# A macaron block on one core: key products of rows 6 to 15 as two f16 products, new places for part of the work, weights fetched earlier

## What is computed

```python
def ffn(x):                                # on layernorm(x); all weights are -1, 0 or 1, with a scale per output
    h = silu(tlin(x, w1, w1_s)) * tlin(x, w2, w2_s)          # 256 -> 1024
    h = gelu(tlin(h, h1, h1_s)); h = gelu(tlin(h, h2, h2_s)) # 1024 -> 1024, twice
    return tlin(h, w3, w3_s)                                 # 1024 -> 256

def attention(x):                          # on layernorm(x), and normed once more inside
    q, k, v, beta_pre = split(normed @ w_qkvb + b_qkvb, 4)
    k = k / max(norm(k), 1e-6); beta = sigmoid(beta_pre)
    for t in range(T):                     # one state S of 16x16 for each head
        S = S + (beta[t] * (v[t] - S @ k[t])) outer k[t]
        o[t] = S @ q[t]
    return x + o @ w_out + b_out

x = x + 0.5 * ffn(layernorm(x)); x = x + attention(layernorm(x)); x = x + 0.5 * ffn(layernorm(x))
```

## Time and profile before

| | |
|---|---|
| median of 3 runs | 1837.86 us (1837.82 to 1837.88) |
| the profiled execution's own time | 1835.54 us |
| its span, first to last instruction | 1833.8 us |
| PE busy | 1764.8 us, 96% |
| PE weight loads busy | 1063.5 us, 58% |
| DVE busy | 1249.4 us, 68% |
| POOL busy | 1075.2 us, 59% |
| ACT busy | 989.1 us, 54% |
| granted PE clock | 0.997 of full speed |

### The profile page before, as it was taken

The page is one execution under the profiler, slowest core; times in us unless marked ns, Lnnn a source line. Parts: engine busy times, 40 slices in busy tenths (PEclk is TensorE's granted clock), DMA queues, the critical chain, the costliest instruction groups (busy, mean ns, idle before and its releaser), DMA issues.

```text
span 1833.8 us, 28121 instructions
## 1 busy us (share of the span) xinstructions
PE 1764.8 (96%) x9674; PEld 1063.5 (58%) x9674; DVE 1249.4 (68%) x2873; ACT 989.1 (54%) x1904; POOL 1075.2 (59%) x1314
## 2 busy tenths in 40 slices
PE   5999999999999999999999999999999899999999
PEld 3865555555655555555555556555555555555588
DVE  5365687777776876767677686767868777778441
ACT  4555464555555454655545465554646454645454
POOL 3553574647465655747466574755756575657563
PEclk8999999999999999999999999999999999999999
DMA  7100000000000000000000000000000000000000
GB/s 273 56 1 1 1 1 1 1 1 1 1 1 1 24 1 12 13 1 2 0 24 1 1 1 1 24 1 1 1 1 1 1 1 12 1 1 13 1 13 13
DMA packets 5260, 23.05 MB, mean 13 GB/s; under 512 B 640, under 2 KB 1664, under 8 KB 3584
## 3 DMA queue, kind: packets, MB, share of 16 engines
q1 hardware_dynamic: 5120, 21.26, 3.1%
HBM read 17.06 MB, written 4.19 MB: 12 GB/s over the span
## 4 chain that ended last, share of the span: by engine, by line
PE 80%; DVE 7%; issue 6%; POOL 4%; ACT 3%; DMA 0%; DVEq 0%; POOLq 0%; SPq 0%; ACTq 0%
PE ffn_bank L1030 46%; PE ffn_bank L1013 10%; PE att_bank L1078 6%; PE att_bank L1050 5%; PE att_bank L1068 5%; PE state_bank L1086 2%; PE ln_bank L981 2%; POOL hid_lo L520 2%; PE att_bank L1065 1%; POOL pairs L549 1%; PE att_bank L1066 1%; PE att_bank L1095 1%; ACT hid L637 1%; DVE roots L756 1%; DVE qk_u L842 1%
## 5 line engine op out<-in xcount | busy, mean ns | idle before, releaser
L1030 PE MATMUL ffn_bank<-hid_hi,w_sb 128*128 128x512 f16 (+1 forms) x2592 | 893.6, 356 | 11.7 <-DVE w_sb L727 5.6
L1030 PE MATMUL ffn_bank<-hid_lo,w_sb 128*128 128x512 f16 (+1 forms) x2592 | 893.4, 356 | 0.0
L520 POOL TENSOR_TENSOR hid_lo<-hid,hid_hi 128x512 f16<-128x512 f32 (+1 forms) x432 | 454.4, 1068 | 385.0 <-ACT hid_hi L613 383.8
L1030 PEld LDWEIGHTS ffn_bank<-hid_hi,w_sb 128*128 128x128 f16 x2592 | 262.9, 101 | 222.3 <-issue 18.3
L549 POOL TENSOR_TENSOR pairs<-KQ 128x32 f32<-128x32 f32 (+15 forms) x496 | 324.6, 667 | 113.5 <-DVE KQ L805 57.2
L1030 PEld LDWEIGHTS ffn_bank<-hid_lo,w_sb 128*128 128x128 f16 x2592 | 254.1, 98 | 228.4 <-issue 26.7
L613 ACT CAST hid_hi<-hid 128x512 f16<-128x512 f32 (+1 forms) x432 | 231.5, 572 | 32.9 <-DVE hid L778 32.5
L637 ACT ACTIVATE hid<-ffn_bank,par_sb 128x512 f32<-128x512 f32 (+1 forms) x288 | 169.0, 637 | 148.3 <-PE ffn_bank L1030 146.8
L1013 PE MATMUL ffn_bank<-xn_hi,w_sb 128*128 128x512 f16 (+1 forms) x576 | 200.2, 357 | 13.9 <-DVE w_sb L727 6.3
L557 POOL TENSOR_TENSOR pairs_lo<-pairs,pairs_hi 128x32 f16<-128x32 f32 (+15 forms) x256 | 180.5, 711 | 52.1 <-ACT pairs_hi L685 47.2
L1013 PE MATMUL ffn_bank<-xn_lo,w_sb 128*128 128x512 f16 (+1 forms) x576 | 200.0, 357 | 0.0
(11 more groups left out here) (82 smaller groups left out, 2092.7 us busy)
## 6 DMA issues: line engine op xcount, KB each, us to landing
NK<-in_w SPq DMA_DIRECT2D x11, 1024.0 KB, 5.0
X<-in_x SPq DMA_DIRECT2D x7, 512.0 KB, 3.6
out<-X SPq DMA_DIRECT2D x7, 512.0 KB, 2.6
wqkvb_sb<-in_wqkvb SPq DMA_DIRECT2D x1, 1024.0 KB, 10.1
X<-in_x SPq DMA_DIRECT2D x2, 256.0 KB, 2.7
out<-X SPq DMA_DIRECT2D x2, 256.0 KB, 2.1
wout_sb<-in_wout SPq DMA_DIRECT2D x1, 256.0 KB, 11.2
par_sb<-in_par SPq DMA_DIRECT2D x1, 24.0 KB, 2.5
```

Of the source, the lines that this page charges most:

```text
L520: pool.tensor_tensor(hid_lo[layer % 2][:, m, call.cols], hid[:, u % 3, call.cols], hid_hi[layer % 2][:, m, call.cols], ALU.subtract).then_ ...
L1030: mm = nc.tensor.matmul(ffn_ps(call, j), weight(name, kk, 2 * pair + i), v[:, kk, cols], start=kk == 0 and part == 0, stop=kk == KT_FF - 1 ...
```

## The change

1. kk rows 6 to 15 are made as qk rows are: a high part by ACT, a low part by POOL, and two f16 products on PE, with a new f16 matrix `head_minus16`. Rows 1 to 5 stay in f32.
2. The place of each pairs, high and low instruction is no longer a fixed distance from PE's tick alone. A loop over all products puts the pairs of a cut product 9 ticks ahead, the high part 4 and the low part 3, and later where the product before it or the owner of its buffer would come later (`MAKE_AT`, `HIGH_AT`, `LOW_AT`).
3. Tables move: the last chunk's opening product from tick 66 to 69 and its update from 81 to 82, the tenth qk row from 26 to 23, the output projection from 53 to 52, one step of the attention norm, and four feed-forward norms by 1 to 3 ticks. ACT copies the keys 8 ticks after a chunk opens, not 6.
4. At the start SP no longer waits for x: three pieces of weights follow the parameters at once, and the second half of x comes after them. The second layer norm moves to slots 26 to 66 of the first call. DVE casts a piece after every second `mix`, and PE waits for a piece of h1, h2 or w3 only at the slot that uses it. ACT calls Sqrt once on a constant before anything else.

```diff
-FIRST_TICK = 2
+FIRST_TICK = 0
-E_RETR = [0, 22, 44, 66]
-E_STATE = [13, 35, 58, 81]
+E_RETR = [0, 22, 44, 69]
+E_STATE = [13, 35, 58, 82]
-E_OUT = 53
+E_OUT = 52
-E_QK = [1, 4, 6, 10, 12, 14, 17, 19, 21, 26, 28, 32, 34, 36, 39, 41]
+E_QK = [1, 4, 6, 10, 12, 14, 17, 19, 21, 23, 28, 32, 34, 36, 39, 41]
-PAIR_LEAD = {"kk": 4, "qk": 9}
+PAIR_LEAD = {"whole": 4, "half": 9}
-SPLIT = {use: q for q, use in enumerate(u for u in DOTS if u[0] == "qk")}
+SPLIT_FROM = {"kk": 6, "qk": 0}
+SPLIT = {use: q for q, use in enumerate(u for u in DOTS if u[2] >= SPLIT_FROM[u[0]])}
...
+MAKE_AT, HIGH_AT, LOW_AT = {}, {}, {}
+for _q, _dot in enumerate(DOTS):
+    _last = DOTS[_q - 1] if _q else None
+    _at = max(WHEN[_dot] - PAIR_LEAD["half" if _dot in SPLIT else "whole"], FIRST_TICK - TICKS, MAKE_AT.get(_last, -TICKS))
+    if _q >= PAIR_BUFFERS:
+        _owner = DOTS[_q - PAIR_BUFFERS]
+        _at = max(_at, LOW_AT[_owner] if _owner in SPLIT else WHEN[_owner])
+    MAKE_AT[_dot] = _at
+    if _dot in SPLIT:
+        _i = SPLIT[_dot]
+        _at = max(WHEN[_dot] - HIGH_LEAD, _at, HIGH_AT.get(SPLITS[_i - 1], _at) if _i else _at)
+        if _i >= HALF_BUFFERS:
+            _at = max(_at, WHEN[SPLITS[_i - HALF_BUFFERS]] + 3)
+        HIGH_AT[_dot] = _at
+        LOW_AT[_dot] = max(WHEN[_dot] - LOW_LEAD, _at, LOW_AT.get(SPLITS[_i - 1], _at) if _i else _at)
...
-LN_SECOND = dict(sum=2, mean=4, square=6, sq_sum=8, var=10, root=12, apply=30, low=34)
+LN_SECOND = dict(sum=26, mean=30, square=32, sq_sum=36, var=40, root=43, apply=62, low=66)
...
+            load_head(0)
+            sp.dma_start(par_sb[:, :], par).then_inc(par_loaded, 16)
             for i in range(W_PIECES):
                 stage_piece(i)
+                if i == W_STAGES - 1:
+                    load_head(1)
...
+            act.wait_ge(eps_ready, 2)
+            act.activation(gate[:, 0, 0:1], eps[:, 0:1], ACT.Sqrt)
...
+            nc.vector.tensor_scalar(head_minus16[:, :], head_ones[:, :], -1.0, None, ALU.mult).then_inc(side_ready, 1)
...
-                        if e == E_RETR[c] + 6:
+                        if e == E_RETR[c] + 8:
                             make_kz(f, c)
...
                 if pair == 0:
+                    if n == 0:
+                        pe.wait_ge(w_ready, -(-(W_AT[name][0] + (kk + 1) * (W_AT[name][1] // KT_FF)) // W_PIECE))
...
-                    i = SPLIT[dot]
-                    nc.tensor.matmul(ps[:, 0:n], head_ones16[:, :], pair(pairs_hi, i, dot), start=True, stop=False)
-                    nc.tensor.matmul(ps[:, 0:n], head_ones16[:, :], pair(pairs_lo, i, dot), start=False, stop=True).then_inc(att_filled, 1)
+                    i, ones = SPLIT[dot], head_ones16 if dot[0] == "qk" else head_minus16
+                    nc.tensor.matmul(ps[:, 0:n], ones[:, :], pair(pairs_hi, i, dot), start=True, stop=False)
+                    nc.tensor.matmul(ps[:, 0:n], ones[:, :], pair(pairs_lo, i, dot), start=False, stop=True).then_inc(att_filled, 1)
```

More of the change, by code:

```diff
@@ L155, in dots_at @@
         f, e = f + 1, e - TICKS
-    found = [("qk", f - 1, t) for t in range(C) if E_QK[t] == e and 1 <= f <= PARTS]
-    return found + [("kk", f + 1, t) for t in range(1, C) if E_KK[t] == e and f + 1 < PARTS]
-USES = []
+    found = [("kk", w, t) for w, at in ((f, e + TICKS), (f + 1, e)) for t in range(1, C) if E_KK[t] == at and 0 <= w < PARTS]
+    return found + [("qk", f - 1, t) for t in range(C) if E_QK[t] == e and 1 <= f <= PARTS]
+USES, WHEN = [], {}
 for _f in FRAMES:
@@ L169 @@
         USES += dots_at(_f, _e)
+        WHEN.update({dot: _f * TICKS + _e for dot in dots_at(_f, _e)})
         if _f >= 1 and _e == E_OUT:
@@ L293, in build @@
         x_loaded, par_loaded, att_w_loaded, stored = (sem(n) for n in ("x_loaded", "par_loaded", "att_w_loaded", "stored"))
+        x_head = [sem(f"x_head{h}") for h in range(HALVES)]
         w_staged = [sem(f"w_staged{i}") for i in range(W_STAGES)]
@@ L559, in attention @@
             def attention(f, e):
[L560 to L566, removed]
+                for dot in DOTS_BY[2].get(f * TICKS + e, ()):
+                    low_pairs(dot)
+                for dot in DOTS_BY[0].get(f * TICKS + e, ()):
+                    make_pairs(dot)
             def alone(call, job, second):
@@ L917, in attention @@
                         key_scale(f + 1)
-                for dot in dots_at(f, e - 1) if e else ():
+                if f >= 1 and e == E_OUT + 2:
+                    add_out(f - 1)
+                for dot in dots_at(f, e - 1):
                     if dot[0] == "qk":
@@ L945, in alone @@
                         convert(i)
-                    mix(call, 0)
-                    mix(call, 1)
+                    for i in range(2, 2 + KT_FF // 2):
+                        mix(call, 2 * i - 4)
+                        mix(call, 2 * i - 3)
+                        convert(i)
                     ln("center", second)
-                    for i in range(2, 5):
-                        mix(call, 2 * i - 2)
+                    for i in range(2 + KT_FF // 2, W_PIECES - 2):
                         convert(i)
-                        mix(call, 2 * i - 1)
                     ln("recip", second)
                     ln("norm", second)
-                    for i in range(5, W_PIECES):
+                    for i in range(W_PIECES - 2, W_PIECES):
                         convert(i)
@@ L1019, in ffn @@
                 if kk == 0:
-                    if pair == 0:
-                        loaded(name)
                     for i in range(2):
```

42 lines of the change are left out of this document (20 added, 22 removed).

## The result

The changed kernel takes 1827.57 us (median of 4 runs, 1826.43 to 1830.87) against 1837.87 us before: 0.9946 times the time [0.9931 to 0.9961]. That is 10.3 us less, where 23.9 us were forecast. It lies inside the range, but fewer than half of the forecast gain came, and the experiments show that it came from another place: the split of the kk rows, the core of the forecast, costs 7.3 us, and the start and the moved steps pay for it.

A forecast was written before the change was run, and what follows sets the result against it. PE, busy 96% of the span, was taken as the bound. Split 43.7 - 38 + 9.8 = 15.5 us and start 7.5 us off 1835.54 gave 1812.5 us profiled, 1814 us as median; range for 8 in 10: 1786 to 1831 us.

The forecast's parts named there:

- the start: Before h1: table loads and casts leave the chain, h1 starts at about 28 us; 7.5 us less, range 3 to 9.
- the moved steps: qk row 9, output projection, attention norm, key copies moved 1 to 3 ticks: costed at nothing, bound -6 to +6 us.
- the 38 us: PE's new waits for kk low parts, from POOL's queue in the stretch, summed over parts; bounds 10.7 and 52 us.
- old waits: Waits of the old kk products, 5.8 us for pairs and 4.0 us for DVE, go: 9.8 us.
- Shorter products: kk rows 6 to 15 on PE: 0.39 us less per 480 columns, 2.73 us a part, 43.7 us in 16 parts.
- New waits, by kind of part: PE's waits: six long parts 2.0 us each, six short 3.2, parts 4, 7, 14 none, part 0 7 us.
- The place of `xn_lo`: On POOL, row 11's low part stands behind `xn_lo`, which in a short part waits through `xn_hi` for DVE's norm.
- The lock: POOL and DVE lock each other out; POOL holds each of 14 wide norms up, estimated 14 x 0.8 = 11 us.
- rival D: At the start: if the weights bound it, early fetch gives up to 5 us more, inside the range; no chance given.
- A: POOL keeps up: kk low parts cost what qk's cost, 10.7 us of waits; 1787.6 us; 22%.
- B: The split gives nothing: waits reach 52 us and only the start's gain is left; 1830 us; 14%.
- C: Last chunk's chain: DVE comes late for its update in every part; at 2 us each 1846 us; 5%.

The follow-up runs named there:

- experiment 1: The changed kernel without the split: all kk rows left in f32, start, tables and order as changed; 1820.29 us, 0.9903.
- experiment 4: The kernel before with the edits of the start alone, tables and split as before; 1829.77 us, 0.9957.
- experiment 6: The changed kernel with `xn_lo` at tick 84 in eleven frames, behind the kk rows, same work; 1811.68 us, 0.9853.
- experiment 9: The changed kernel with `xn_lo` at tick 84 in eleven frames and no kk row split; 1818.72 us, 0.9897.
- 2: The changed kernel with kk low parts computed for 32 columns only, the rest left out; 1808.01 us, 0.9837.
- experiment 8: The changed kernel with DVE's feed-forward norm computed for 32 columns instead of 512 in the frames; 1816.48 us, 0.9881.
- experiment 7: The changed kernel with kk pairs, high and low parts one tick earlier, low parts four ticks ahead; 1831.90 us, 0.9961.
- 12: The changed kernel with `xn_lo` at tick 84 in eleven frames and kk low parts of 32 columns only; 1799.50 us, 0.9789.

## Why the prediction was right in the mechanism and wrong in the size

The step that failed is the net cost of the split's waits, 38 - 9.8 = 28.2 us; experiment 1 against the changed kernel shows some 53 us. That alone makes the split a loss. The queue on POOL, from which the 38 us came, is not what failed: kk low parts made PE wait 39.7 us. What failed is what the sum put at nothing. The clock fell behind the waits (10 us), kk rows waited for DVE's `NK` too (8.8 us), and 3.1 of the 9.8 us of old waits go without the split, by the moved steps. Next to it, "I cost them at nothing" for the moved steps was 9.5 us of gain, which covers the loss in part.

| term | forecast | measured | by |
|---|---|---|---|
| shorter kk products | -43.7 | about -43 | PE busy, 1 against after, clock taken out |
| waits for kk low parts | +38 | +39.7 | PE's waits, after |
| other waits of kk rows (`NK` 8.8, ACT 0.7) | 0 | +9.5 | PE's waits, after |
| old waits of kk rows | -9.8 | -6.7 | PE's waits, 1 |
| half clock behind waits | 0 | +10 | the five stretches |
| start | -7.5 | -8.2 | 4 |
| moved steps and order | 0 (-6 to 6) | -9.5 | 4 to 1 |
| total of medians | -23.9 | -10.3 | |

The four rows of waits and clock come to 52.5 us, and 43.1 + 10 = 53 us by PE's idle time. With it the column adds up to some -8 us and not to -10.3: the rows of waits and clock are from the profiled executions, and that of the changed kernel is the slowest of its four, 3.3 us above their median. By medians the split is +7.3 us, by spans +10.2.

**Shorter products.** Right: 0.41 for 0.80 us. PE's busy time fell by 34.3 us and not by the 40 that the prediction names, because the half clock lengthens what is left.

**New waits, by kind of part.** The idle time of PE just before its kk products, added over the parts (what it waits for low parts alone in brackets): part 0 7.4 us (4.5), 7 forecast; the six long parts 15.1 us (14.3), 12 forecast; the six short parts 22.5 us (20.9), 19 forecast; parts 4, 7 and 14 4.6 us (0, all of it for `NK`), 0 forecast. So the kinds were sized well for low parts. Inside the parts two errors cancel, and that is luck. Row 11 waits 1.58 for 2.0 us and 3.21 for 2.9 in the two parts that were worked through, but over the long parts it waits 6.2 us where 12 were put, and over the short ones 11.8 where 17.4 were. Rows 10, 12 and 13 wait for their low parts 21.2 us, and I gave rows 12 and 13 of a short part 0.3 us and row 10 nothing. A late low part also holds back the list behind it. Part 15 shows it on POOL and on PE:

```profile
1627.01 2.13 POOL L536 TENSOR_TENSOR xn_lo<-xn,xn_hi 128x1024 f16<-128x1024 f32 x1 [2.90 <-ACT xn_hi L633]
1629.10 0.85 POOL L586 TENSOR_TENSOR pairs_lo<-pairs,pairs_hi 128x352 f16<-128x352 f32 x1
...
1630.80 2.26 POOL L549 TENSOR_TENSOR hid_lo<-hid,hid_hi 128x512 f16<-128x512 f32 x2
1633.02 0.91 POOL L586 TENSOR_TENSOR pairs_lo<-pairs,pairs_hi 128x384 f16<-128x384 f32 x1
```

```profile
1630.00 0.32 PE L1092 MATMUL att_bank<-pairs_hi,head_minus 128*128 128x352 f16 x1 [1.54 <-POOL pairs_lo L586]
...
1633.99 0.50 PE L1092 MATMUL att_bank<-pairs_hi,head_minus 128*128 128x384 f16 x1 [2.65 <-POOL pairs_lo L586]
```

A pair of `hid_lo` stands between the low parts of rows 11 and 12, so row 12 waits longer than row 11, and the clock is halved from 1632.1.

**The place of `xn_lo`.** Right as a cause, and not the only one: moving it gives 15.9 us (6), without the split only 1.6 (9), and taking POOL's time for the low parts away gives 19.6 (2). The gate in front of it was wrong for part 3: ACT's `hid_hi`, not DVE's norm.

**The clock.** Missing. "The clock is full" was read from before and carried over, though the forecast itself made PE wait for microseconds. It was not full in before either: 0.997 on average, with 10.2 us at half clock at the start. 10 us of the 25 us by which the cost was undersized can be read there. That the waits cause it is the reading of where the stretches lie; no run changes the clock alone.

**The lock.** The prediction let POOL hold DVE's norm and estimated 11 us for it, outside the sum. The 14 wide norms take 1.58 us on average after the change and 1.39 before, and some 1.22 in the parts where they are shortest: 5 us of holding in all and not 11. In part 9 it also went the other way: the norm held the pair of `hid_lo` for a microsecond (3.25 for 2.27 us, experiment 8), and was itself 2.12 us long. The queue of POOL should have had that in it. The Trainium skill (SBUF — State Buffer, Who interferes with whom) calls the port pair that DVE and POOL share an exclusive lock; the trace agrees, in both directions, with the 3.25 us here and the 1.12 us of the short norm in experiment 8.

**The start.** Right: the second norm's table loads left the way to h1, while the first w1 product stayed at 16.89 us (16.68 before), so the early fetch itself gave nothing there and rival D is out. Two things that the 7.5 us did not hold nearly cancel. h1 starts 8.5 us earlier and now at full clock, where before it ran at half clock until 40.0, which cost 2.3 us. And 1.7 us came back at 39.87, where PE waits for POOL's part of the second norm.

**Moved steps.** I took the 0 between two bounds, and the gain lies beyond the better one. PE is idle 8.6 us less in experiment 1 than in experiment 4 (55.5 and 64.1 us): waits for kk pairs 5.8 to 3.7 us, for `NK` 4.0 to 2.9, for `Uz` 4.6 to 3.5, and several small ones of the feed-forward; another 3.2 us of the difference of these two profiles are clock. Which table gives which was not tried.

**Rivals.** A is out: low parts wait 50.3 us and not 10.7. B's statement on the split, that the new waits take back all it saves, is what happened, and more: a net cost of 53 us with the clock, where B took 43.7. Its 1830 us would be 1837 by the measured loss of 7.3 us, and the moved steps made it 1827.6. C is out at 8.8 us for `NK` and 3.0 for `Uz`, but is the next in line: experiment 7 ran into it.

**What stays open.** With `xn_lo` late and POOL's new work nearly gone the split yields 19.2 us (9 to 12) of some 43. PE is idle 76.0 us there and 54.2 in experiment 9. It waits 10.7 us for DVE's `NK` and 13.4 us for kk low parts: 7.2 us of these for low parts right behind a pair of `hid_lo`, which in five of six places had itself waited for ACT's `hid_hi`, and 4.1 us behind an `xn_lo` that experiment 6 leaves in place (parts 0 and 5). No run takes these away one by one.

## What to carry to other kernels

Where one engine's list runs in order and feeds the bounding engine, work out the wait of every item of the stretch and not of the worst alone: what is late once is late again behind the next large item. Before splitting work onto such an engine, look for what stands in front of it in its list that nobody needs yet: here one table entry for `xn_lo` turned a loss of 7 us into a gain of 7. Put a price on the clock where a change makes that engine wait. And measure each part of a change alone; this one was faster as a whole while its core was slower.

## What the runs showed of the hardware

- PE at 95% busy fell to a granted clock of 0.50 in five stretches of 3.4 to 6.8 us. Ahead of each, or across its start, PE had waited for a low part; from start to start, less the product's own time, the longest of these waits were 4.3, 3.4, 1.75, 2.0 and 2.8 us. Products of 512 columns then start every 0.43 us instead of 0.22. Experiment 1, whose longest wait for a low part is 1.5 us, has none in its parts. Against a plain rule: the kernel before had a wait of 2.5 us and in its profile no such stretch in the parts, and experiment 4, with the same longest wait, had two of 3.4 us. The changed kernel has a wait of 2.15 us in part 5 with the clock at full behind it:

```profile
602.78 0.32 PE L1092 MATMUL att_bank<-pairs_hi,head_minus 128*128 128x352 f16 x1 [2.15 <-POOL pairs_lo L586]
```

- The four runs of the changed kernel differ by 4.4 us (1826.43 and 1826.50 at a mean clock of 0.996, 1828.63 at 0.994, 1830.87 at 0.993), those of experiment 1 by 1.1 us, all at 1.000. The spread goes with the clock.
- A DVE product of two SBUF tiles and a POOL subtraction that run together both get longer: 2.12 us where the shortest of the same shape take some 1.22, and 3.25 us where it is 2.27 with a short product beside it.
